# Expert-choice layer of an audio tower: feed-forward on gathered chosen tokens, expert sums as products with token marks

## The reference

```python
# B, L, H, E, F, C = (8, 2048, 128, 8, 256, 2) is written there; here b = 16, l = 748, h = 128, e = 8
k = min(max(int(l * C / e), 1), l)                 # 187 of 748 tokens for each expert
S = jax.nn.softmax(x @ Wg, axis=-1)
G, I = jax.lax.top_k(jnp.swapaxes(S, 1, 2), k)     # the expert chooses its tokens
ex = jnp.take_along_axis(x[:, None], I[..., None], axis=2)
hmid = gelu(einsum('bekh,ehf->bekf', ex, W1) + b1)  # exact gelu, F = 256
out = einsum('bekf,efh->bekh', hmid, W2) + b2
vals = G[..., None] * out
new_x = zeros_like(x).at[batch, I].add(vals)
```

## Time and profile before

| | us |
|---|---|
| median of three runs | 2936.68 (2932.05 to 2938.7) |
| the profiled execution, its own time | 2933.99 |
| its span, first to last instruction | 2932.2 |
| PE busy | 2627.6 (90%) |
| DVE busy | 2230.6 (76%) |
| ACT busy | 1926.7 (66%) |
| POOL busy | 1188.3 (41%) |

### The profile page before, as it was taken

How to read it: one execution, slowest core, us unless ns; L and a number is a source line. 1 busy time by engine, 2 the same in 40 slices (tenths; PEclk the granted TensorE clock), 3 DMA queues, 4 the chain that set the end, 5 groups by cost and what they waited for, 6 DMA issues and landing times. The chain is left out here.

```text
span 2932.2 us, 55307 instructions
## 1 busy us (share of the span) xinstructions
PE 2627.6 (90%) x17000; PEld 2050.1 (70%) x17000; DVE 2230.6 (76%) x3615; ACT 1926.7 (66%) x3292; POOL 1188.3 (41%) x1160
## 2 busy tenths in 40 slices
PE   8979799999999997589999999788856997999993
PEld 7969454444444445489999999688845885888882
DVE  4545689999999984769999998577766664777875
ACT  3336277777777786378888887344445885777772
POOL 0034012323232324345555555333234776466664
PEclk9989699999999998589999999899988998999997
DMA  3109433333333320622222333500002111577748
GB/s 81 36 27 371 94 57 57 56 56 56 56 56 56 56 39 1 201 75 89 85 87 84 88 85 79 197 1 0 0 1 87 50 47 64 176 250 237 251 156 251
DMA packets 148619, 278.24 MB, mean 95 GB/s; under 512 B 27836, under 2 KB 80805, under 8 KB 141576
## 3 DMA queue, kind: packets, MB, share of 16 engines
q1 hardware_dynamic: 134920, 251.89, 31.4%
q0 software_dynamic: 13568, 24.75, 2.5%
HBM read 190.89 MB, written 87.11 MB: 95 GB/s over the span
## 5 line engine op out<-in xcount | busy, mean ns | idle before, releaser
L1049 ACT ACTIVATE probs<-score 128x748 f32<-128x748 f32 (+1 forms) x768 | 568.4, 794 | 116.4 <-PE score L874 115.0
L978 DVE TENSOR_REDUCE part_max<-to_dve 128x1 f32<-128x512 f32 (+1 forms) x768 | 480.2, 684 | 82.8 <-PE to_dve L855 82.2
L2726 DVE TENSOR_TENSOR m_hid_lo<-m_hid,m_hid_hi 128x512 fp32r<-128x512 f32 x408 | 289.2, 710 | 158.2 <-ACT m_hid_hi L2699 158.2
L1522 DVE TENSOR_TENSOR f_hid_lo_c<-f_hid_c,f_hid_hi_c 128x748 fp32r<-128x748 f32 x256 | 350.4, 1378 | 42.1 <-ACT f_hid_hi_c L1505 38.8
L855 PE MATMUL to_dve<-k_stack,q_stack 48*128 48x512 f32 (+3 forms) x1536 | 351.6, 367 | 20.2 <-DMA k_stack<-k_parts 19.3
L1418 POOL TENSOR_TENSOR f_acc_c<-f_acc_c,f_gate_c 128x748 f32<-128x748 f32 x112 | 252.9, 2258 | 259.5 <-DVE f_gate_c L1538 259.2
L874 PE MATMUL score<-q_stack,k_stack 49*128 49x374 f32 (+1 forms) x1536 | 317.5, 389 | 3.1 <-ACT probs L1049 1.0
L874 PEld LDWEIGHTS score<-q_stack,k_stack 49*128 49x128 f32 (+1 forms) x1536 | 162.0, 181 | 225.0 <-ACT probs L1049 199.7
L1500 ACT ACTIVATE f_hid_c<-f_up_c,c_b 128x374 f32<-128x374 f32 x512 | 268.5, 571 | 76.1 <-DVE f_hid_lo_c L1522 52.0
L911 PE MATMUL o_sum<-probs,v_sb 128*17 128x374 f32 (+1 forms) x3072 | 315.6, 483 | 0.1
L2622 POOL DMA_INDIRECT e_sums<-m_gated,m_row_in x216 | 213.0, 986 | 162.0 <-DVE m_gated L2744 108.6
(11 more groups left out here) (431 smaller groups left out, 6496.9 us busy)
## 6 DMA issues: line engine op xcount, KB each, us to landing
m_weights<-e_records SPq DMA_DIRECT2D x54, 1028.0 KB, 7.0
f_gate_c<-c_gates SPq DMA_DIRECT2D x128, 374.0 KB, 3.4
q_stack<-q_parts SPq DMA_DIRECT2D x192, 93.5 KB, 3.1
k_stack<-k_parts SPq DMA_DIRECT2D x192, 93.5 KB, 4.3
e_slots<-blank SPq DMA_DIRECT2D x54, 260.0 KB, 3.8
m_row_in<-e_slots SPq DMA_DIRECT2D x54, 260.0 KB, 2.9
m_weights<-e_sums SPq DMA_DIRECT2D x16, 640.0 KB
e_records<-l_parts SPq DMA_DIRECT2D x16, 512.0 KB, 3.6
```

What stands on the lines that cost most here:

```text
L978: dve.tensor_reduce(part_max[0:ROWS[c], k, j, c, 0:1], ring[i % RING][0:ROWS[c], :], AX.X, ALU.max).then_inc(used, 1)
L1049: act.activation(probs[0:n, s % 2, m, 2 * j:2 * j + 2, :], score[tile][0:n, :, 0:HALF], ACT.Exp).then_inc(tile_used, 1)
L1522: dve.tensor_tensor(hid_lo[:, k % RING, :], hid[:, k % 2, :], hid_hi[:, k % RING, :].bitcast(F32), ALU.subtract).then_inc(lo_done, 1)
L2726: dve.tensor_tensor(hid_lo[:, f % RING, :], hid[:, f % RING, :], hid_hi[:, f % RING, :].bitcast(F32), ALU.subtract).then_inc(lo_done, 1)
```

## The change

`route` becomes `choose`, `gated_ffn` becomes `chosen_ffn`, and `router_logits` also writes its normalised rows to memory.

- `router_logits`: `r_rows` has four slots; SyncE writes each sequence's rows (768 x 128 values) into `c_rows` in memory, 136 values a row; a slot is reused when it has been turned and written.
- `choose`: ScalarE's queue writes the probabilities into the last 8 values of each row of `c_rows` (16 DMAs, 12,288 pieces of 32 bytes). After the 24 rounds, the chosen tokens are replaced by a key (748 less the token's number), and a second series of rounds (24 MAX8, 23 MATCH_REPLACE8) lists the keys of each expert in 192 slots (187 chosen, five empty). They are turned by TensorE; VectorE keeps the keys and the row numbers `ids`.
- `chosen_ffn`: a unit is one pair of experts of one sequence: 2 x 192 = 384 slots, three tiles of 128; there are 64 units. GpSimd gathers the three tiles by indirect DMA (ring of five units) and builds the third of three mark matrices (128 slots by 748 tokens, 1 where the slot's token is the column's); VectorE builds the other two. TensorE turns the rows (3 transposes), does 12 matmuls of 192 columns up and 12 down, turns back (3), and adds the unit into the sequence's sums in PSUM by 18 matmuls (`combine`: six token tiles by three slot tiles, marks as weights, 256 columns: gated rows' high and low part). The gate is applied by ScalarE (high part, 4 instructions) and VectorE (low, 4). Once in four units VectorE adds the sums to `h` (`give_back`, 8 instructions) and takes statistics (`measure`, 6).

The order in which each engine meets the units is written out by hand. The core of the diff:

```diff
+        R_RING = 4
...
+            if keep is None and b >= R_RING:
+                eng.wait_ge(turned, b - R_RING + 1)
+                eng.wait_ge(saved[b % R_RING], 16 * (b // R_RING))
...
+                        sp.dma_start(save[b * TILES * P:(b + 1) * TILES * P, 0:P].rearrange("(c p) d -> p c d", p=P),
+                                     rows_of(b)).then_inc(saved[b % R_RING], 16)
...
-def route(nc, g, logits, gates, k_tokens, k_experts, tag, later):
+def choose(nc, g, logits, rows, ramp, keys_at, ids, k_tokens, tag, later):
...
-                dve.scalar_tensor_tensor(out=gate_cols[:, :], in0=work[:, :], scalar=0.0, in1=cols[:, :],
-                                         op0=ALU.is_lt, op1=ALU.mult).then_inc(whole, 1)
+                then(dve.scalar_tensor_tensor(out=work[:, :], in0=work[:, :], scalar=0.0, in1=ramp[:, :],
+                                              op0=ALU.is_lt, op1=ALU.mult))
+                for r in range(SLOTS_E // 8):
+                    some = key[:, 8 * r:8 * r + 8]
+                    then(dve.max(some, work[:, :]))
+                    if r < SLOTS_E // 8 - 1:
+                        then(dve.match_replace(work[:, :], some, work[:, :], -1.0))
+                then(dve.tensor_copy(key[:, SLOTS_E:WHOLE], key[:, 0:WHOLE - SLOTS_E]))
...
-def gated_ffn(nc, g, w1_hi, w1_lo, b1, w2_hi, w2_lo, b2, shared_b2, blocks, shared, gates, out, tag):
+def chosen_ffn(nc, g, w1_hi, w1_lo, b1, w2_hi, w2_lo, b2, rows, ramp, keys_at, ids, tag):
...
+        POOL_TILE, MARK_BEHIND = 2, 3
...
+                for k in range(UNITS_C + MARK_BEHIND):
+                    if valid(k):
+                        gather(k)
+                    if valid(k - MARK_BEHIND):
+                        mark(k - MARK_BEHIND)
...
+                def combine(n, tiles):
+                    b, i = divmod(n, PER_BATCH)
+                    pe.wait_ge(gated_n, n + 1)
+                    pe.wait_ge(marked, (UNIT_TILES - 1) * (n + 1))
+                    pe.wait_ge(pool_marked, n + 1)
+                    for c in tiles:
+                        if i == 0 and b and c % 2 == 0:
+                            pe.wait_ge(added, BANKS * (b - 1) + c // 2 + 1)
+                        for j in range(UNIT_TILES):
+                            last = pe.matmul(sums[c // 2][0:ROWS[c], c % 2, :, :], marks[:, n % 2, j, c * P:c * P + ROWS[c]],
...
+                for k in range(-1, UNITS_C + 2):
+                    if valid(k):
+                        widen(k)
+                    if valid(k - 1):
+                        narrow(k - 1)
+                    if valid(k - 2):
+                        combine(k - 2, range(0, TILES // 2))
+                    if valid(k + 1):
+                        turn_rows(k + 1)
+                    if valid(k - 2):
+                        combine(k - 2, range(TILES // 2, TILES))
+                    if valid(k - 1):
+                        turn_back(k - 1)
...
+                def gate_rows(n):
+                    dve.wait_ge(gate_hi, GATES * (n + 1))
...
+                    done = k - 3 if valid(k - 3) and (k - 3) % PER_BATCH == PER_BATCH - 1 else None
+                    if valid(k - 2):
+                        gate_rows(k - 2)
+                    if done is not None:
+                        give_back(done // PER_BATCH)
+                    if valid(k - 1):
+                        mark(k - 1, 0)
+                    if valid(k):
+                        split_hid(k, 0)
+                    if valid(k - 1):
+                        mark(k - 1, 1)
+                    if valid(k):
+                        split_hid(k, 1)
+                    if valid(k + 1):
+                        split_x(k + 1)
+                    if done is not None:
+                        measure(done // PER_BATCH)
```

More of the change, by code:

```diff
@@ L1260, in _ @@
-                rounds = -(-k_tokens // 8)
-                for r in range(rounds):
+                then(dve.tensor_copy(work[:, 0:512], turn[:, 0, :]))
+                then(dve.tensor_copy(work[:, 512:T], turn[:, 1, 0:T - 512]))
+                for r in range(-(-k_tokens // 8)):
                     then(dve.max(best[:, :], work[:, :]))
@@ new lines, in chosen_ffn, with experts_of, gate_parts, gate_of @@
+        gathered = [sem(f"f_gathered{k}") for k in range(RING)]
+        GATES = 4
+        POOL_TILE, MARK_BEHIND = 2, 3
+        def experts_of(n):
+            return [2 * (n % PER_BATCH) + e for e in range(2)]
+        def gate_parts(n):
+            one, two = experts_of(n)
+            return [(slice(0, P), 0, one), (slice(0, H), 1, one), (slice(H, P), 1, two), (slice(0, P), 2, two)]
+        def gate_of(n, part):
+            at, tile, e = part
+            return row_in[at, n % RING, tile, P + e:P + e + 1]
@@ L1542, in takes @@
-                def takes(b, slot, k):
-                    if ends(k):
-                        take(b, slot, item_of(k))
-                def give_back(b, part):
-                    dve.wait_ge(turned_back, b * 2 + (part + 1))
-                    for c0, c1, n in [(0, 3, P)] if part == 0 else [(3, 5, P), (5, 6, LAST)]:
-                        h = g.h[0:n, bass.ds(b * TILES + c0, c1 - c0), :]
-                        last = dve.tensor_tensor(h, h, back[0:n, c0 % 3:c0 % 3 + (c1 - c0), :], ALU.add)
-                    last.then_inc(returned, 1)
-                    if out is None:
-                        dve.wait_ge(returned, b * 2 + (part + 1))
-                        take_statistics(dve, g, b, range(3 * part, 3 * part + 3))
@@ new lines, in mark, with give_back @@
+                def mark(n, j):
+                    b, i = divmod(n, PER_BATCH)
+                    if n >= 2:
+                        dve.wait_ge(combined, n - 1)
+                    dve.tensor_scalar(marks[:, n % 2, j, :], ramp[:, :], keys_at[:, b, i, j:j + 1], None, ALU.is_equal
+                                      ).then_inc(marked, 1)
+                def give_back(b):
+                    dve.wait_ge(combined, PER_BATCH * (b + 1))
+                    PARTS_B = [(0, 2, P), (2, 4, P), (4, 5, P), (5, 6, LAST)]
+                    for half in range(2):
+                        if half:
+                            dve.wait_ge(half_added, b + 1)
+                        for c0, c1, n in PARTS_B:
+                            h = g.h[0:n, b * TILES + c0:b * TILES + c1, :]
+                            last = dve.tensor_tensor(h, h, sums[c0 // 2][0:n, c0 % 2:c0 % 2 + c1 - c0, half, :], ALU.add)
+                            if half and c1 % 2 == 0:
+                                last.then_inc(added, 1)
+                        if not half:
+                            last.then_inc(half_added, 1)
@@ L1578, in load_small @@
+                give_back(B - 1)
+                measure(B - 1)
 def load_small(nc, loads, tag):
```

469 lines of the change are left out of this document (212 added, 257 removed).

## The result

The changed kernel takes 2848.14 us (median of four runs, 2847.14 to 2850.41) against 2935.99 us of the kernel before in the same comparison: a ratio of 0.9703, 95% interval 0.9686 to 0.972. The profiled execution spans 2845.1 us, 87.1 less than before.

What follows compares the result with a forecast made beforehand. TensorE, busy 565 of 586 us, was taken to bound `gated_ffn`, and VectorE's rounds to set the end of `route`. 2934 + 34 (choice) - 134 (layer) + 0 + 0 = 2834 us, range 2790 to 2897.

Steps and rivals of the forecast that it cites:

- The router's write-out: In `router_logits`: writing each sequence's rows to memory costs 0 us, the last write being covered; uncovered it would cost 3.2.
- the small pieces: In `choose`: 12,288 pieces of 32 bytes taken as 0 us; rival that they clog the DMA engines, +18 us, chance 0.05.
- The choice, +34: In `choose`: the second series and the operations behind it open the next block at 1285.1 us, +34 us, nothing hiding it.
- One unit 6.8 us: In `chosen_ffn`: mean time per unit, from three units of 6.1 and one of 8.6 us, 6.7, plus small waits.
- Loop 1: In `chosen_ffn`: `turn_back` waits behind the previous unit's `combine`, which needs its gates; one turn 5.95 us.
- Loop 2: In `chosen_ffn`: VectorE's marks and splits after the gates, then TensorE's widening and narrowing before the next combine: 6.1 us a unit.
- The turn with `give_back`, 8.6 us: In `chosen_ffn`, once in four units: VectorE's `give_back` ahead of the splits and `measure` behind them, 8.6 us from gates to gates.
- 24 + 63 x 6.8 = 452: Whole `chosen_ffn`: 18 us to the first combine, 6 behind the last, 63 units between; 452 instead of 586 us, -134.
- TensorE at its lower clock for the whole layer: Rival in `chosen_ffn`: TensorE stays at 1.2 GHz, a unit takes 8.8 us, total 2960 us; chance 0.08.
- Tighter loops: Rival in `chosen_ffn`: `give_back` fits into slack and marks are cheap, 6.0 to 6.3 us a unit, 2784 to 2803 us; chance 0.12.
- GpSimd or its memory: Rival in `chosen_ffn`: GpSimd or memory shared with VectorE decides, 7.3 to 7.8 us a unit, 2866 to 2897 us; chance 0.23.
- TensorE waits mostly for VectorE's gates and splits: Sign expected in the profile after, in `chosen_ffn`: TensorE's waits mostly on VectorE's gates and splits; no size given.

Runs made afterwards that it cites:

- e7: Changed kernel with the second series' 23 MATCH_REPLACE8 left out, so each round lists the same eight tokens: ratio 0.9621 to the kernel before.
- e4: Changed kernel with VectorE's two marks made by a two-input instruction of the same size instead of the one-input one: 2847.52 us, ratio 0.9699.
- e2: Changed kernel with `give_back` placed ahead of the next unit's gates in VectorE's order instead of behind them: 2813.72 us, ratio 0.9579.
- e5: Changed kernel with all three marks made by VectorE and none by GpSimd: 2846.63 us, ratio 0.9686.
- e3: Changed kernel with TensorE's `turn_back` between the two halves of the previous unit's `combine` instead of behind both: 2813.26 us, ratio 0.9577.
- c1: Changed kernel with `give_back` ahead of the gates and `turn_back` between the halves of `combine`, next rows turned ahead of both halves: ratio 0.9558.

## Why the prediction was right, and where its steps were not

- **The router's write-out, 0, and the small pieces, 0: right.** VectorE waits 1.83 us at the start of `choose` and waited 1.13 at that of `route`, which is all that the last write can have cost: 0.7 us, and `choose` begins at 1174.36 for 1174.16. The queue with the 32-byte pieces (q10, 12,544 packets) took 0.2% of the 16 engines' span of 2845 us, about 6 us of a stretch of 111. The bound of 18 us is excluded by the opening at 1285.35.
- **The choice, +34: right, to 0.3 us**, in its parts too: 24 MAX8 at a pitch of 2.01, an end of VectorE at 1282.5 (1283.1 forecast), 2.1 us to the next block. e7 confirms that nothing hides it. One premise was off: the later weights, said to end before 1250, now end at 1258.3, which still leaves 24 us.
- **One unit 6.8 us: right in the mean (6.83), wrong in the parts, so in part by luck.** Loop 1 was taken at 5.95 and is 6.28 to 6.30: the combine with its transposes 2.58 instead of 2.45, the gates 1.76 and 1.34 instead of 1.65 and 1.2, the hand-overs the rest. Loop 2 was taken at 6.1 a unit with marks of 0.94 us (its 3.5 and 2.7 add up to 6.2 and not 6.3, which leaves 6.1), and it doesn't set the pace: the marks take 0.60, and in e4 even 0.99 lengthened only the turn behind `give_back`, by 0.35. The estimate by the Trainium skill (VectorE: DVE Perf Modes, "The perf-mode tier table"), 0.55 us, was the better price, and the conclusion drawn from it, 19 us less, was wrong, since loop 1 doesn't contain the mark.
- **The turn with `give_back`, 8.6 us: the mechanism was wrong.** I had it as VectorE's list from gates to gates. It is TensorE's `combine` that waits for the bank, 2.13 us where an ordinary turn has 0.54 of idle time: 7.87 us. That it ends near my 8.6 is luck: it is due to something I had not priced, a fall of TensorE's clock after 7 of the 15 waits, 1.5 us each. e2 removes both with two lines.
- **"24 + 63 x 6.8 = 452" is the step that missed: the 24.** The stage took 464.4 us (1285.3 to 1749.7). From the opening (its first gather) to the first combine it is 24.5 us for my 18, and behind the last combine's start 9.7 for my 6, because the last units have nothing beside them, so TensorE idles and the combine runs at the lower clock (4.21 us instead of about 2.6). 6.5 + 3.7 us, and 1.7 in the turns, are the 12 us between -134 and -122; the rest of the 14 is 1 us in the later layers and 1 between profile and median.
- **The rivals.** TensorE at its lower clock for the whole layer: no, 0.97. Tighter loops: no, 6.3 us is the loop's floor and not an average with slack. GpSimd or its memory: not in this kernel (e5), but 0.04 to 0.6 us a unit away, and it took over in e3 and c1. A mark of VectorE that begins within GpSimd's takes up to 2.33 us (e3), against 0.60 alone, and ends 0.4 us after GpSimd's. The Trainium skill (SBUF — State Buffer, "Who interferes with whom") has it as a lock that whoever issues first keeps for its whole instruction, the other being blocked. The traces agree on the blocking. On who comes first they don't by the recorded starts: in c1 29 marks of VectorE begin 0.01 to 0.18 us before GpSimd's, and it is VectorE's that take 2.59 to 2.77 us. In the changed kernel 31 marks of VectorE also begin within one of GpSimd, but 30 of them more than 2.0 us into its 2.18, where nothing is left to wait for. That TensorE waits mostly for VectorE's gates and splits was half right: 27.8 us for gates, 32.0 for `give_back`, 4.3 for the splits.

## What to carry to other kernels

Where four engines share a unit with 5.3 to 6.2 us of work each, write down the loops and the floors under them in order: here loop 1 (6.3), GpSimd's list (6.2) and TensorE (5.5), with the waits at a sequence's change on top. An edit that frees a floor is worth nothing until the loop above it is gone: a mark moved off GpSimd brought 0 us alone and 14 to 19 us after the two reorderings (with VectorE's list in another order too). And price the first and the last units apart from the steady ones, because nothing covers their chain and TensorE's clock was low there (0.58 in the first 25 us, 0.50 in the last combine).

## What the runs showed of the hardware beyond that

- A wait of 2.13 us in a TensorE otherwise 90% busy was followed by the lower clock in 7 of 15 cases, with nine 256-column matmuls in 2.26 us instead of 1.33; one of 0.54 us never was in the steady part of the changed kernel. With waits of 1.73 us (e4) it was 4 cases, and with 0.75 (e3) none.
- A one-input VectorE `tensor_scalar` over 748 f32 values takes 0.60 us, and the two-input `scalar_tensor_tensor` of e4 0.99. In e3 the first one took 2.33 us when it began 0.26 us into a `tensor_scalar` of GpSimd, and 1.25 when it began 1.34 us into one. The second took its 0.99 us in all 31 such cases of e4, one of them 1.21 us in, where the other form would have needed 1.4. The same section of the Trainium skill says that an instruction with two SBUF inputs contends with a GpSimd instruction that reads SBUF; on VectorE's side these 31 rows don't show it, though 30 of them meet only the last 0.4 us. What they show is the other side: where the two-input mark was under way first, GpSimd's took 2.53 to 2.56 us instead of 2.18, 11 times. c1 with two-input marks would be the test of which form is better there; it wasn't run.
- GpSimd's indirect gather takes 0.94 us alone, and in the changed kernel 1.27 to 1.86 for nearly all that lie beside a mark of VectorE. With two-input marks (e4) such gathers take 0.95 to 1.54, and with all marks on VectorE (e5) hardly one takes more than 1.07, so a mark beside it isn't the whole cause; what is isn't settled.
- A `tensor_scalar` of GpSimd over 748 values took 2.18 us (2.07 by the slope of small ones).
